# Moving the LSTM cell work of a language-model tower one gate unit later, and two loads behind the first rows

## What is computed

```python
h = tok(x)                            # embedding of 89 columns, and 39 columns from an STFT of the one-hot ids
h = h + attn(layernorm(h))            # 8 heads: 64 summary tokens and a window of 17 tokens
h = h + ffn(layernorm(h))

# ffn: the router picks K=2 of E=8 experts for each token; each expert is an LSTM over the 16 rows
gates = xt @ Wi + h @ Wh + b
i_, f_, g_, o_ = jnp.split(gates, 4, axis=-1)
c = jax.nn.sigmoid(f_) * c + jax.nn.sigmoid(i_) * jnp.tanh(g_)
h = jax.nn.sigmoid(o_) * jnp.tanh(c)
y = h @ Wo + bo
```

## Time and profile before

| | us |
|---|---|
| median of 3 runs (lowest to highest) | 1795.67 (1794.84 to 1796.5) |
| the profiled execution | 1793.76 |
| its span | 1792.0 |
| PE busy | 1672.9 (93%) |
| VectorE busy | 1541.5 (86%) |
| ScalarE busy | 1002.6 (56%) |
| mean granted TensorE clock, share of full | 0.978 |

### The profile page before, as it was taken

The page is one execution under the profiler, slowest core; times in us unless marked ns, Lnnn a source line. Parts: engine busy times, 40 slices in busy tenths (PEclk is TensorE's granted clock), DMA queues, the critical chain, the costliest instruction groups (busy, mean ns, idle before and its releaser), DMA issues.

```text
span 1792.0 us, 25559 instructions
## 1 busy us (share of the span) xinstructions
PE 1672.9 (93%) x9722; PEld 813.6 (45%) x9722; DVE 1541.5 (86%) x2418; ACT 1002.6 (56%) x1124; POOL 48.8 (3%) x42
## 2 busy tenths in 40 slices
PE   4376999999999999999999999999999999999998
PEld 2233444444444444444444444444444444444443
DVE  3679898989989898898989989898898989989865
ACT  3245656556565655656556565655656556555644
POOL 1000000000000000000000000000000000000000
PEclk9578999999999999999999999999999999999999
DMA  3132412314132232312314132232422324143221
GB/s 122 23 77 61 86 51 59 67 53 79 40 77 59 50 74 55 71 52 58 67 53 79 40 79 57 50 75 53 71 53 57 67 55 78 40 80 57 56 60 33
DMA packets 204091, 110.94 MB, mean 62 GB/s; under 512 B 125796, under 2 KB 185111, under 8 KB 203968
## 3 DMA queue, kind: packets, MB, share of 16 engines
q1 hardware_dynamic: 203888, 109.28, 28.0%
q10 hardware_dynamic: 80, 0.02, 0.0%
HBM read 89.84 MB, written 4.74 MB: 53 GB/s over the span
## 4 chain that ended last, share of the span: by engine, by line
PE 54%; DVE 30%; issue 9%; ACT 4%; SPq 1%; DMA 1%; POOL 0%; DVEq 0%; ACTq 0%; POOLq 0%
PE gates L543 41%; DVE tmp L1052 4%; PE yp L549 3%; DVE C L1056 3%; DVE tmp L1067 2%; DVE Hs L1036 2%; ACT tmp L694 2%; DVE xm L1024 2%; DVE tmp L1046 2%; PE FA L482 2%; PE FA L467 2%; DVE z L1071 1%; SPq L303 1%; DVE tmp L1031 1%; DVE xn L837 1%
## 5 line engine op out<-in xcount | busy, mean ns | idle before, releaser
L694 ACT ACTIVATE tmp<-gates,bias_sb 128x1024 f32<-128x1024 f32 x504 | 559.1, 1110 | 466.9 <-PE gates L543 465.7
L543 PE MATMUL gates<-xm,wi_sb 128*128 128x512 f16 x3024 | 739.7, 381 | 5.0 <-ACT tmp L694 5.0
L543 PE MATMUL gates<-Hs,wh_sb 128*128 128x512 f16 x2880 | 699.9, 379 | 0.0
L543 PEld LDWEIGHTS gates<-xm,wi_sb 128*128 128x128 f16 x3024 | 292.4, 99 | 387.6 <-issue 82.1
L543 PEld LDWEIGHTS gates<-Hs,wh_sb 128*128 128x128 f16 x2880 | 281.7, 98 | 339.9
L701 ACT ACTIVATE tmp<-C 128x1024 f32<-128x1024 f32 x128 | 135.2, 1056 | 171.1 <-DVE C L1056 168.7
L1046 DVE SCALAR_TENSOR_TENSOR tmp<-tmp 128x1024 f32<-128x1024 f32 x120 | 145.4, 1212 | 72.6 <-ACT tmp L694 72.6
L1031 DVE SCALAR_TENSOR_TENSOR tmp<-tmp 128x1024 f32<-128x1024 f32 x128 | 156.4, 1222 | 42.8 <-ACT tmp L701 41.0
L1036 DVE SCALAR_TENSOR_TENSOR Hs<-tmp,Hs 128x1024 f16<-128x1024 f32 x120 | 146.9, 1224 | 13.8 <-ACT Hs L705 13.8
L1024 DVE TENSOR_TENSOR xm<-xs,masks 128x2048 f16<-128x2048 f16 x128 | 155.9, 1218 | 2.2 <-DMA masks<-mask_scratch 2.2
L1056 DVE SCALAR_TENSOR_TENSOR C<-tmp 128x1024 f32<-128x1024 f32 x120 | 147.0, 1225 | 4.1
(11 more groups left out here) (157 smaller groups left out, 1172.3 us busy)
## 6 DMA issues: line engine op xcount, KB each, us to landing
masks<-mask_scratch SPq DMA_DIRECT2D x128, 256.0 KB, 5.3
roww<-mw_scratch SPq DMA_DIRECT2D x128, 256.0 KB, 3.7
rowk<-mask_scratch SPq DMA_DIRECT2D x128, 128.0 KB, 2.9
diag<-pr SPq DMA_DIRECT2D x64, 112.0 KB, 3.1
diag<-vwin SPq DMA_DIRECT2D x64, 112.0 KB, 3.1
out_dram<-h SPq DMA_DIRECT2D x16, 256.0 KB, 2.3
C<-in_wi SPq DMA_DIRECT2D x1, 2048.0 KB, 11.0
C<-in_wh SPq DMA_DIRECT2D x1, 2048.0 KB, 15.9
```

What stands on the lines that cost most here:

```text
L543: last = mm(gates[:, slot, k * SEQ:(k + 1) * SEQ], w, v, start=(i < K), stop=(i >= len(seq) - K))
L694: A(tmp[:, gate_at(gate, e), :], gates[:, (n - 1) % 2, :], ACT.Tanh, bias=bias_sb[:, e, gate:gate + 1], scale=UNSCALE).then_inc(s_tanh, 1)
```

## The change

Six things are done at once. (1) VectorE: `cell(e)` moves from unit 4e+2 to 4e+4, `hidden(e)` from 4e+4 to 4e+5, `hidden_lo(e)` from 4e+5 to 4e+7, `input_part(e)` from 4e+1 to 4e+2, `chosen(e)` from 4e+6 to 4e+7. (2) ScalarE: `cell_tanh(e)` moves from 4e+3 to 4e+4, `split_hi(e)` from 4e+4 to 4e+6. (3) TensorE: `unit_y(e)` moves from 4e+8 to 4e+9. (4) `tmp` has an eighth place, so that F and O have two each; tanh of C goes to the expert's own F place, and the chosen rows are weighted into the free half of the O place instead of `z32`; the waits are set to match. (5) `proj` moves from unit 16 to 17, `projT` from 17 to 18. (6) SyncE issues the ids before `wi`, and `wh` and `wo` after the encoder's rows. The core of the diff:

```diff
-    PE_AT = dict(emb=-5, xT=-2, qkv=-1, summary=2, window=4, feature=10, values=15, proj=16, projT=17, x2T=20,
+    PE_AT = dict(emb=-5, xT=-2, qkv=-1, summary=2, window=4, feature=10, values=15, proj=17, projT=18, x2T=20,
...
-            return {I: e % 2, G: 2 + e % 2, F: 4, O: 5 + e % 2}[gate]
+            return {I: 0, G: 2, F: 4, O: 6}[gate] + e % 2
...
+            load(ids, x_ids[0:1, :].to_broadcast([VOCAB, SEQ]), S["ids"])
             load(wi_st.rearrange("p a (b n) -> p (a b) n", b=2), wi.rearrange("e i n -> i e n"), s_wi_load)
-            load(wh_st.rearrange("p a (b n) -> p (a b) n", b=2), wh.rearrange("e i n -> i e n"), s_wh_load)
-            load(wo_sb[:, :, :], wo.rearrange("e i n -> i e n"), s_wo_load)
-
-            load(ids, x_ids[0:1, :].to_broadcast([VOCAB, SEQ]), S["ids"])
             sp.wait_ge(s_enc_sb, 2)
             load(table[ENC0:ENC0 + NFR, D_EMB:D], encA[0:NFR, :], S["enc"])
             load(enc_dram[0:P, :], encA, s_enc_out)
             load(enc_dram[P:NBJ, :], encB, s_enc_out)
+            load(wh_st.rearrange("p a (b n) -> p (a b) n", b=2), wh.rearrange("e i n -> i e n"), s_wh_load)
+            load(wo_sb[:, :, :], wo.rearrange("e i n -> i e n"), s_wo_load)
...
-                    if g == 0 and e >= 2:
+                    if g == 1 and e >= 2:
                         unit_y(s, e - 2)
...
-                    if g == 0 and e and not last:
+                    if g == 0 and e:
+                        cell_tanh(s, e - 1)
+                    elif g == 0 and not first:
+                        cell_tanh(s - 1, E - 1)
+                    if g == 2 and e and not last:
                         split_hi(s, e - 1)
...
-                    if g == 3:
-                        cell_tanh(s, e)
                     run_front(front, t, s)
...
-                    if g == 0 and e:
-                        hidden(s, e - 1)
+                    if g == 0 and e and not first:
+                        cell(s, e - 1)
...
-                    if g == 1 and e and not last:
+                    if g == 3 and e and not last:
                         hidden_lo(s, e - 1)
...
-                    if g == 2 and e:
+                    if g == 3 and e:
                         chosen(s, e - 1)
...
                     run_front(lambda u, b: front(u, b, b % 2), t, s)
-                    if g == 1:
+                    if g == 1 and e:
+                        hidden(s, e - 1)
...
+                    if g == 2:
                         input_part(s, e, first)
-                    if g == 2 and not first:
-                        cell(s, e)
```

More of the change, by code:

```diff
@@ L88, in lm_tower_kernel @@
         Hs = sb("Hs", [P, E, 2, K * SEQ], f16)
-        tmp = sb("tmp", [P, 7, K * SEQ])
+        tmp = sb("tmp", [P, 8, K * SEQ])
         masks = sb("masks", [P, 2, K, SEQ], f16)
@@ L392, in step @@
                     e, g = t // NG, t % NG
-                    if t == 9 and not first:
+                    if t == 10 and not first:
                         store(s - 1, 1 - par)
@@ L548, in unit_y @@
                 pe.wait_ge(s_z, s * E + e + 1)
-                mm(yp[:, :], wo_sb[:, e, :], z32[:, :], start=False, stop=(e == E - 1)).then_inc(s_y, 1)
+                mm(yp[:, :], wo_sb[:, e, :], chosen_at(e), start=False, stop=(e == E - 1)).then_inc(s_y, 1)
             def y_bias(s):
@@ L571, in step @@
                         unit_gate(s, e, g, first)
-                    if g == 0 and e == 2:
+                    if g == 1 and e == 2:
                         y_bias(s)
-                    if g == 0 and e >= 2:
+                    if g == 1 and e >= 2:
                         unit_y(s, e - 2)
-                    elif g == 0 and not first:
+                    elif g == 1 and not first:
                         unit_y(s - 1, e - 2 + E)
@@ L687, in gate_tanh @@
                 m = s * E + e
-                if gate == F and m >= 1:
-                    act.wait_ge(s_h, m)
+                if gate == F and m >= 2:
+                    act.wait_ge(s_h, m - 1)
                 elif gate == O and m >= 2:
-                    act.wait_ge(s_z, m - 1)
+                    act.wait_ge(s_y, m - 1)
                 elif m >= 2:
@@ L698, in cell_tanh @@
                 act.wait_ge(s_c, s * E + e + 1)
-                if s == 0 and e:
-                    act.wait_ge(s_h, e)
-                A(tmp[:, TANH_C, :], C[:, e, :], ACT.Tanh, scale=0.5).then_inc(s_tc, 1)
+                if s == 0 and e >= 2:
+                    act.wait_ge(s_h, e - 1)
+                A(tmp[:, gate_at(F, e), :], C[:, e, :], ACT.Tanh, scale=0.5).then_inc(s_tc, 1)
             def split_hi(s, e):
@@ L755, in _ @@
             run_steps(step_p)
+            cell_tanh(STEPS - 1, E - 1)
             y_out(STEPS - 1)
@@ L1030, in hidden @@
                 at = tmp[:, gate_at(O, e), :]
-                STT(out=at, in0=at, scalar=1.0, in1=tmp[:, TANH_C, :],
+                STT(out=at, in0=at, scalar=1.0, in1=tmp[:, gate_at(F, e), :],
                     op0=ALU.add, op1=ALU.mult).then_inc(s_h, 1)
@@ L1101, in step @@
                     run_front(lambda u, b: front(u, b, b % 2), t, s)
-                    if g == 1:
+                    if g == 1 and e:
+                        hidden(s, e - 1)
+                    elif g == 1 and not first:
+                        hidden(s - 1, E - 1)
+                    if g == 2:
                         input_part(s, e, first)
-                    if g == 2 and not first:
-                        cell(s, e)
+                    if t == XM_AT and not last:
+                        masked_input(s + 1, 0, 1 - par, False)
             dve.wait_ge(s_pad, 1)
@@ L1119, in _ @@
             run_steps(step)
+            cell(STEPS - 1, E - 1)
             hidden(STEPS - 1, E - 1)
```

22 lines of the change are left out of this document (9 added, 13 removed).

## The result

The changed kernel takes 1813.62 us (median of 4 runs, 1812.08 to 1814.34) against 1795.7: a ratio of 1.0099, 95% interval 1.0081 to 1.0116. It is slower by 18 us, and above the predicted range of 1788 to 1803. Its profiled execution has a span of 1810.3 us, 18.3 more than before.

The account below looks back on a forecast made before the run. TensorE, all but always busy in steady state, was taken as the bound. 1793.76 - 5.5 (start) - 3.4 (step 0) + 10.5 (14 steps) = 1795.4, or 1797.3 in the median's terms, given as 1797; range 1788 to 1803.

Parts of the forecast that it names:

- the steady state: Term for the 14 steps with a whole front: +0.75 us a step, +10.5 us; ends -2.8 and +21.
- step 0: Term where VectorE sets the pace: two TensorE waits, 2.83 and 2.28 us, shrink; -3.4 us, ends 0 and -5.1.
- the start: Term for the loads: ids ahead of wi, front's first matmul at 24.0 instead of 29.45; -5.5 us.
- Steps 1 and 3: After gate unit 6: hidden_lo(0) starts at 2.29; ScalarE's cell_tanh(3), tanh and copy behind proj are done at 40.18.
- Step 2: VectorE works without a gap from hidden_lo(0) until cell(3) is done: 35.07 us, ending at 37.36.
- Step 4: Behind projT, VectorE's moments2 to xn2 let x2T start at 47.89; PE wants it at 45.85, waits 2.0 us.
- Step 5: From x2T through the logits, with 0.2 us more wait: unit 22 starts at 52.83, 0.8 us later than before.
- The stretch: TensorE's time from the end of gate unit 6 to the start of unit 22: 52.02 us before, 52.83 predicted.
- VectorE's gapless stretch is longer: Rival, chance 0.25: reordered pairs on VectorE wait for each other; 1800 us, or 1808 at +1.5 a step.
- all 2.5 us of waits of a step: Far case of the rival that the cell chain isn't late: x2T doesn't wait either; 1752 us, chance 0.02.
- no wait of L499: Sign in steady state: TensorE's wait for attn before proj, at most 1.5 us before, is gone.
- the 0.95 us at unit 15: Sign in steady state: TensorE waits about 0.9 us at unit 15 for the tanh of unit 13.

Follow-up runs that it names:

- the two fillers: e3 and e10: eight spare matmuls ahead of TensorE's wait at x2T, added to the changed kernel and to e4; 1804.48 and 1782.94 us.
- e6: The changed kernel with proj and projT put back to units 16 and 17; 1821.72 us.
- e1: The kernel before with SyncE's new order of the loads alone; 1788.09 us.
- e5: The kernel before with proj and projT alone one unit later; 1773.6 us.
- e8: The kernel before with proj and projT one unit later and the new order of loads, no move of the cell work; 1766.15 us.
- e9: e8 with x2T, the logits, x_lo, the choice and the weights one unit later; 1755.05 us.
- e11: e9 with the front's parts at their old units in step 0; 1756.71 us.
- e3: The changed kernel with eight spare matmuls ahead of TensorE's wait at x2T, in step 0 too; 1804.48 us.
- e10: e4 with the eight spare matmuls of e3 ahead of TensorE's wait at x2T; 1782.94 us.
- e4: The changed kernel with split_hi(0) ahead of the tanh of unit 6 on ScalarE; 1799.6 us.
- e2b: e2 with the front's two copies of unit 20 ahead of cell_tanh(4) on ScalarE; 1792.48 us.
- e2: The changed kernel with xn2 ahead of hidden_lo(3) and chosen(3) on VectorE; 1840.33 us.

## Why the prediction was wrong

I put 1797, and it is 1813.6. In spans I had +1.6 us and it is +18.3. The missing 16.7 are: 6.4 in the steady state, 6.2 by the clock, and 4.4 in step 0, less 0.3 that the start gave more than I had.

- **Steps 1 and 3 right.** `hidden_lo(0)` at 2.29 behind the end of gate unit 6 (1081.00 less 1078.71), as predicted to the hundredth, with VectorE idle for 2.65 where I had 2.8. ScalarE then takes 2.69 from the start of `cell_tanh(3)` to `projT` (1116.55 to 1119.24), where step 3 has 2.70. The rest of the step, from unit 22 on, is 55.45 us in both kernels (interval less stretch), as assumed.
- **Step 2 failed by its size.** I put 35.07 us for the gapless stretch. It is 35.43 (1081.00 to 1116.43). The instructions are those counted; what was missed is their neighbours. `hidden_lo` stood ahead of the front's work or of `input_part`, and the next began 1.13 to 1.15 behind it in all 14 steps. Now `chosen` of the same expert follows it, and begins 1.32 to 1.34 behind (1081.00 to 1082.33 here). I put this down to `chosen`'s wait for `hidden_lo`'s own semaphore (`s_hlo`): behind `input_part`, where it stood before and where that semaphore had long come, it began after 1.08 to 1.14 in the step that I follow. No run takes that wait out. With `chosen`'s second instruction 0.07 sooner behind the first, that is 0.12 per pair. Three pairs lie in the stretch, 0.36 us. The rival had named this: "`hidden_lo` before `chosen` ... wait for each other in new places". I had dismissed it with "1 us or more of room", which is true of waits for another engine and not of one between neighbours of the same queue.
- **Step 4 right in what it predicts, late by what it takes over.** `x2T` waits 1.98 us (2.0 predicted) at 48.34 (47.89): 0.36 from step 2 and 0.1 from a fourth pair (1123.19 to 1124.51). **Step 5** gives 4.88 where I had 4.94. The stretch is 53.22, I had 52.83, and then took 0.75 a step instead of the 0.8 of my own sum. 1.21 less 0.75, 14 times, is the 6.4 us.
- **What no step of mine has: the clock.** I priced a 2.0 us wait at 2.0 us. In four steps it cost 1.56 more. The 14 steps of before don't show it, since no wait of them is over 1.5 us and none is followed by a long step. But step 0 of the same trace does: behind a wait of 1.98 us a row of six matmuls took 2.74 us instead of 1.46, at a granted clock of 0.50 (timeline and window of PE, before):

```profile
169.01 2.74 PE L543 MATMUL gates<-xm,wi_sb 128*128 128x512 f16 x6 [1.98 <-ACT tmp L694]
170.00:172.00 2.00, 2.00 (x8) 0.88 (x6) 2.00 (x2) 1.71 (x2) 0.00 (x0) 0.50 0.03 8
```

That the wait is the cause of the long steps is shown by the two fillers: same order, same chain, no long steps.

- **Step 0: -3.4 predicted, not found.** The two waits that I looked at did shrink, from 2.83 to 1.93 us and from 2.28 to 1.14. But VectorE sets the pace there (busy for 9.8 of every 10 us from 110 to 140), so the time went to other waits: the one at `x2T` grew from 3.24 to 4.58 us, `unit_y` waits three times for 0.65 to 1.89, and a gate unit 2.68 for a tanh. From the first gate unit of step 0 to that of step 1 it is 84.53 against 83.52 before. Whether that 1.0 us is a loss by the change isn't shown. Step 0 took 82.73 to 84.96 us in the traces of the other kernels with the late cell work (e6 apart), and 83.90 to 85.44 in e1, e5, e8, e9 and e11 without it. Only e6 stands out with 88.71. What makes the rest is open in the main; the clock seems to have a part in it. The filler, which runs in step 0 too, goes with a shorter step 0 (83.50 in e3 against 84.53, 82.73 in e10 against 84.96 in e4) and a higher granted clock from 140 to 183 us (0.92 and 0.96 against 0.88). The step that failed is taking two waits of an engine that isn't the bound as gain.
- **The start: right, -5.8 for -5.5** at the first gate unit. The first matmul of the front starts at 23.05 where I had 24.0, 2.0 us after the row's issue at 21.02. The later `wh` held nobody up: it landed 8.3 us after its issue at 22.91, and ScalarE used it from 42.68 on. The Trainium skill (DMA: Bandwidth & Descriptors, section on queues, rings and completion order) has it that each DMA engine takes the descriptors of a ring in order, which puts the row behind `wi`. From that I worked out that it could not start before 21.7 and the gain would be 5.0. The front gained 6.40, so the 5.0 was too low. The trace neither bears the rule out nor refutes it. Without `wh` beside it most of `wi` was through sooner: the DMA engines' busy share is 0.48 from 18 to 19 us and 0.06 from 19 to 20, where it was 1.04 or more before. Yet the page of the profile puts `wi`'s landing at 11.0 us after its issue in both kernels, which is 22.0 here. The row took 2.0 us against the 2.5 of the small transfer in the earlier trace rows, so no delay by `wi` shows.

Of the rivals, "VectorE's gapless stretch is longer" came true, with the mechanism it names; I gave it 0.25 and its far end 1808. The clock and step 0 lie outside every case I had. Two sizes were misread from the kernel before: "all 2.5 us of waits of a step" are 2.0 (27.8 us in 14 steps), and the wait at `x2T` was 0.38 us and not "about 0.5". Also right: no wait of L499, and the 0.95 us at unit 15.

## What to carry to other kernels

Before a part of the order is moved, ask of each move alone what wait it removes: here one move of a small matmul had all of the gain in the steps, and the larger one, which went with it, took back nearly twice as much. When an instruction gets a new neighbour in the same queue, look whether it reads or waits for what the neighbour writes, and add that to each such pair. In a kernel like this one, price a wait of TensorE of some 2 us above its length (here by 1.6 to 1.7 us where the clock fell), and in a stage where another engine is the bound count no wait of TensorE as gain.

## What was not expected of the hardware

One idle stretch of 1.98 us in an engine that is otherwise busy for 100 us was enough to lower TensorE's granted clock to 0.50, but not each time: behind the same wait it fell in 4 of 14 steps in the changed kernel and in 10 of 14 in e4, at 1.55 to 1.56 us each. Behind the 2.0 us at `attn` in e6 it fell in 2 of 14 steps. What decides in which steps it falls is open. Behind waits of 0.87 and 0.96 us (e2b, 28 of them) or 1.5 us (before, 14) there was no long step; behind 2.56 us (e2) 8 of 14 were long, and the longest by 3.2 us. The Trainium skill (TensorE: Matmul & The Clock Gate, section on oscillation) describes kernels in which idle stretches between groups of matmuls bring the clock down again and again. The traces agree with that in kind, with one such stretch of 1.98 us in a step. Eight matmuls that compute nothing, put into the idle time, made the kernel 16.7 us faster in e10 (1799.6 to 1782.9).
